# Weights and a context chunk loaded in 32 by 32 blocks and turned by VectorE, in the first stage of an attention kernel

## The reference

```python
x = x + _L0_xattn_ref(_layernorm(x, axis=-1), ctx_1024, ctx_1024, wq, bq, wk, bk, wv, bv, wo, bo)
...
    q = (query @ wq.T + bq).reshape(B, SQ, H, HD).transpose(0, 2, 1, 3)
    k = (key @ wk.T + bk).reshape(B, -1, H, HD).transpose(0, 2, 1, 3)
    v = (value @ wv.T + bv).reshape(B, -1, H, HD).transpose(0, 2, 1, 3)
    scores = jnp.einsum('bhqd,bhkd->bhqk', q, k) / jnp.sqrt(jnp.asarray(HD, q.dtype))
    attn = jax.nn.softmax(scores, axis=-1)
...
x = x + _L0_attn_ref(_layernorm(x, axis=-1), ...)
x = x + _L0_ffn_ref(_layernorm(x, axis=-1), ...)
```

## Time and profile before

| | |
|---|---|
| time, median of 3 runs | 1691.88 us (1691.49 to 1692.56) |
| profiled execution: its time | 1690.8 us |
| profiled execution: span from the first to the last instruction | 1689.0 us |
| TensorE matmul busy | 1619.8 us, 96% |
| VectorE, ScalarE, GpSimd busy | 1179.0, 950.8, 899.7 us |
| first stage: first transpose, first product, last eviction | 6.50, 14.55, 69.57 us |
| mean granted TensorE clock | 0.973 |

### The profile page before, as it was taken

One profiled execution on the slowest core, in us unless ns is written; L12 is line 12 of the kernel. 1 busy time (PEld: TensorE's weight loads), 2 busy tenths in 40 slices (PEclk: granted clock), 3 DMA queues, 4 the chain that ended last, 5 costly groups with the idle time before them and its releaser, 6 DMA issues. The chain is left out here.

```text
span 1689.0 us, 36984 instructions
## 1 busy us (share of the span) xinstructions
PE 1619.8 (96%) x15589; PEld 1314.5 (78%) x15604; DVE 1179.0 (70%) x1523; ACT 950.8 (56%) x1437; POOL 899.7 (53%) x472
## 2 busy tenths in 40 slices
PE   7999999999999999999999999667998899999999
PEld 6788888888888888888888887556886677777787
DVE  5137888888888888888888887877434577653322
ACT  4347776777767777777777776662103677630000
POOL 0026788888878878888887885002000344522220
PEclk9999999999999999999999999788999799899999
DMA  5332222222222222222222210213422111211001
GB/s 187 75 50 35 36 39 40 39 38 37 38 37 42 36 36 40 41 36 37 37 40 37 40 24 5 80 53 113 165 88 94 38 51 51 65 50 50 28 23 50
DMA packets 310404, 88.75 MB, mean 53 GB/s; under 512 B 259392, under 2 KB 292160, under 8 KB 310240
## 3 DMA queue, kind: packets, MB, share of 16 engines
q1 hardware_dynamic: 310240, 86.39, 22.2%
HBM read 71.67 MB, written 14.68 MB: 51 GB/s over the span
## 5 line engine op out<-in xcount | busy, mean ns | idle before, releaser
L655 POOL TENSOR_TENSOR b_acc<-b_acc,b_s 128x1024 f32<-128x1024 f32 x168 | 563.6, 3355 | 12.4 <-ACT b_s L854 5.3
L892 DVE TENSOR_TENSOR b_s<-b_s,b_mb 128x2048 f32<-128x2048 f32 x128 | 398.0, 3111 | 28.4 <-ACT b_mb L837 28.4
L929 DVE TENSOR_TENSOR b_mx<-b_psS,b_mx 128x512 f32<-128x512 f32 x480 | 330.8, 689 | 93.3 <-PE b_psS L720 80.2
L854 ACT ACTIVATE b_s<-b_s 128x2048 f32<-128x2048 f32 x128 | 244.3, 1909 | 18.3 <-DVE b_s L892 15.2
L871 ACT ACTIVATE b_s<-b_psS 128x2048 f32<-128x2048 f32 x128 | 241.2, 1885 | 20.9 <-DVE b_mx L929 20.9
L43 PE MATMUL b_work<-wvT,cT 128*128 128x512 f32 x496 | 202.9, 409 | 0.0
L43 PE MATMUL b_work<-cT,wkT 128*128 128x512 f32 x496 | 200.3, 404 | 1.7 <-POOL b_ones L636 1.7
L44 PE MATMUL b_work<-wvT,cT 128*128 128x512 f32 x496 | 194.5, 392 | 0.0
L44 PE MATMUL b_work<-cT,wkT 128*128 128x512 f32 x496 | 194.2, 392 | 0.0
L45 PE MATMUL b_work<-wvT,cT 128*128 128x512 f32 x496 | 193.8, 391 | 0.0
L45 PE MATMUL b_work<-cT,wkT 128*128 128x512 f32 x496 | 193.4, 390 | 0.0
(11 more groups left out here) (290 smaller groups left out, 2802.4 us busy)
## 6 DMA issues: line engine op xcount, KB each, us to landing
cin<-in_ctx SPq DMA_DIRECT2D x480, 64.0 KB, 2.4
experts_sb<-in_L_ffn_expert_w SPq DMA_DIRECT2D x8, 1024.0 KB, 5.3
q_scratch<-d_st SPq DMA_DIRECT2D x16, 256.0 KB, 2.3
k_scratch<-d_st SPq DMA_DIRECT2D x16, 256.0 KB, 2.3
e_q<-q_scratch SPq DMA_DIRECT2D x16, 256.0 KB, 2.7
k_sb<-k_scratch SPq DMA_DIRECT2D x16, 256.0 KB, 2.9
cin<-in_ctx SPq DMA_DIRECT2D x4, 512.0 KB, 8.4
b_kT<-in_x SPq DMA_DIRECT2D x4, 512.0 KB, 8.0
```

Source lines behind the costliest of these rows:

```text
L655: nc.gpsimd.tensor_tensor(acc[:, :, :], acc[:, :, :], s[:, buf, 2 * i:2 * i + 2, :], ALU.add).then_inc(sum_done, 1)
L854: nc.scalar.activation(part, part, ACT.Exp, scale=SCALE).then_inc(exp_done, 1)
L892: nc.vector.tensor_tensor(s[:, n % BUFS, :, :], s[:, n % BUFS, :, :], mb[:, :].rearrange("p (o n) -> p o n", o=1).broadcast_to([P, CHUNK, ...
L929: nc.vector.tensor_tensor(mx[:, :, :], part, mx[:, :, :], ALU.max).then_inc(mx_done, 1)
```

## The change

The units `("w", 1, k)`, `("w", 2, k)` and `("c", 1, n)` leave `order`. Instead twelve `blocks` (four of wv, four of wq, four of chunk 1) are each loaded with four DMAs by `load_blocks`, turned by VectorE (`turn`) into one of four places in the buffer of wk, copied to the high half by ScalarE at the places that `ahead` lists, and subtracted by GpSimd. The loads of x move ahead of those of wv, and the two bias loads stand behind the sixteen DMAs of wv. VectorE now does all statistics, the rest of the norm and the turning of wv before the normalization of half 0. The square root on ScalarE moves up to the second key unit.

```diff
-        order = ([("w", 0, k) for k in range(KD)] + [("c", 0, n) for n in range(4)]
-                 + [("k", 0, 0), ("w", 1, 0), ("w", 1, 1), ("k", 0, 1), ("w", 1, 2), ("w", 1, 3),
-                    ("k", 0, 2), ("c", 1, 0), ("c", 1, 1), ("k", 0, 3), ("v", 0, 0), ("c", 1, 2), ("c", 1, 3),
-                    ("v", 0, 1), ("w", 2, 0), ("w", 2, 1), ("x", 0, 0), ("x", 0, 1), ("v", 0, 2),
-                    ("w", 2, 2), ("w", 2, 3), ("x", 0, 2), ("x", 0, 3), ("v", 0, 3),
+        order = ([("w", 0, k) for k in range(KD)] + [("c", 0, n) for n in range(4)]
+                 + [("k", 0, j) for j in range(G)] + [("v", 0, 0), ("v", 0, 1), ("x", 0, 0), ("x", 0, 1), ("v", 0, 2),
+                    ("x", 0, 2), ("x", 0, 3), ("v", 0, 3),
...
+        blocks = [("w", 1, k) for k in range(KD)] + [("w", 2, k) for k in range(KD)] + [("c", 1, k) for k in range(KD)]
+        ahead = {("k", 0, 2): blocks[0:2], ("k", 0, 3): blocks[2:4], ("v", 0, 2): blocks[4:6], ("v", 0, 3): blocks[6:8],
+                 ("q", 0, 1): blocks[8:10], ("q", 0, 2): blocks[10:12]}
...
-            load_weights(1)
+            for g in range(G):
+                sp.dma_start(parts[:, g, 1:3, :], x[2 * g:2 * g + 2].rearrange("b p d -> p b d")).then_inc(x_in[g // 2], 16)
+            for u in blocks[0:KD]:
+                load_turned(u)
...
         @block.gpsimd
         def _(pool):
             make_identity(nc, pool, ident, const)
+            for u in blocks:
+                kind, done, count = (("w", w_lo, w_hi), ("c", shared.split_done, shared.hi_done))[u[0] == "c"]
+                pool.wait_ge(count, counted(*u))
+                nc.gpsimd.tensor_tensor(split_place(1, u), turned_place(u), f32(split_place(0, u)),
+                                        ALU.subtract).then_inc(done, 1)
...
-                if (kind, i, j) == ("c", 1, 2):
+                if (kind, i, j) == ("k", 0, 1):
                     norm.scalar(act)
+                for t in ahead.get((kind, i, j), ()):
+                    act.wait_ge(turned, blocks.index(t) + 1)
+                    nc.scalar.activation(split_place(0, t), turned_place(t),
+                                         ACT.Copy).then_inc(w_hi if t[0] == "w" else shared.hi_done, 1)
...
+            def turn(u):
+                n = blocks.index(u)
+                dve.wait_ge(block_in[n], 16 * 4)
+                if n >= 4:
+                    kind, i, j = blocks[n - 4]
+                    dve.wait_ge(w_lo if kind == "w" else shared.split_done, counted(kind, i, j))
+                nc.vector.transpose(turned_place(u), block_place(u)).then_inc(turned, 1)
...
-                if (kind, i, j) == ("w", 1, 2):
+                if (kind, i, j) == ("k", 0, 0):
                     statistics(0)
-                elif (kind, i, j) == ("c", 1, 0):
                     statistics(1)
-                elif (kind, i, j) == ("c", 1, 2):
                     norm.vector(dve)
                     norm.done(dve)
-                elif (kind, i, j) == ("w", 2, 0):
+                    for t in blocks[0:KD]:
+                        turn(t)
                     applied(0)
-                elif (kind, i, j) == ("w", 2, 2):
+                elif (kind, i, j) == ("v", 0, 1):
                     applied(1)
+                    for t in blocks[KD:2 * KD]:
+                        turn(t)
+                elif (kind, i, j) == ("q", 0, 0):
+                    for t in blocks[2 * KD:]:
+                        turn(t)
```

More of the change, by code:

```diff
@@ L214, in context_place, with load_blocks, chunk_columns @@
     return a[:, p % 2, 2 * kk:2 * kk + 2, h * 2 * P:(h + 1) * 2 * P]
-def load_blocks(sp, ctx_in, cin, raw_in, p, k):
-    rows = ctx_in[p // 4, (p % 4) * 512:(p % 4 + 1) * 512, k * P:(k + 1) * P]
+def load_blocks(sp, rows, out, done):
     blocks = rows.rearrange("(t j) (i c) -> i j t c", j=32, i=4)
     for i in range(4):
-        sp.dma_start(cin[32 * i:32 * i + 32, 0, k % 2, :].rearrange("j (t c) -> j t c", c=32),
-                     blocks[i]).then_inc(raw_in[k % 2], 16)
+        sp.dma_start(out[32 * i:32 * i + 32, :].rearrange("j (t c) -> j t c", c=32), blocks[i]).then_inc(done, 16)
+def chunk_columns(ctx_in, p, k):
+    return ctx_in[p // 4, (p % 4) * 512:(p % 4 + 1) * 512, k * P:(k + 1) * P]
 def two(ps):
@@ L248, in queries_and_first_chunk @@
         const = sem("a_const")
+        block_in = [sem(f"a_block_in{n}") for n in range(3 * KD)]
+        turned = sem("a_turned")
         x_in = [sem(f"a_x_in{i}") for i in range(2)]
@@ L281, in queries_and_first_chunk, with turned_place, split_place, block_place @@
         order_of = {kind: [u for u in order if u[0] == kind] for kind in "wcxkvq"}
+        for kind, i, j in blocks:
+            order_of[kind].append((kind, i, j))
+        def turned_place(u):
+            return w_sb[0][:, blocks.index(u) % 4, :]
+        def split_place(a, u):
+            kind, i, j = u
+            return weights[i][1][a][:, j, :] if kind == "w" else cT[a][:, 1, j, :]
+        def block_place(u):
+            kind, i, j = u
+            return w_sb[i][:, j, :] if kind == "w" else cin[:, j // 2, j % 2, :]
         @block.sync
@@ L287, in load_context, with load_turned @@
                              .rearrange("(o p) d -> p o d", p=P)).then_inc(cin_in[h], 16)
-            def load_weights(i):
-                sp.dma_start(w_sb[i], weights[i][0].rearrange("(o p) d -> p o d", p=P)).then_inc(w_in[i], 16)
-            load_weights(0)
+            def load_turned(u):
+                kind, i, j = u
+                rows = weights[i][0][:, j * P:(j + 1) * P] if kind == "w" else chunk_columns(ctx_in, 1, j)
+                load_blocks(sp, rows, block_place(u), block_in[blocks.index(u)])
+            sp.dma_start(w_sb[0], weights[0][0].rearrange("(o p) d -> p o d", p=P)).then_inc(w_in[0], 16)
             for h in range(2):
                 load_context(0, h)
-            load_weights(1)
+            for g in range(G):
+                sp.dma_start(parts[:, g, 1:3, :], x[2 * g:2 * g + 2].rearrange("b p d -> p b d")).then_inc(x_in[g // 2], 16)
+            for u in blocks[0:KD]:
+                load_turned(u)
             with nc.allow_non_contiguous_dma(reason="512 numbers"):
@@ L298, in _ @@
                 sp.dma_start(bq[:, :], w["bq"].rearrange("(g p) -> p g", p=P)).then_inc(b_in, 16)
[L299 to L305, removed]
+            for u in blocks[KD:2 * KD]:
+                load_turned(u)
+            sp.wait_ge(full, place["c", 0, 3] + 1)
+            for u in blocks[2 * KD:]:
+                load_turned(u)
             for k in range(2):
-                load_blocks(sp, ctx_in, cin, shared.raw_in, 2, k)
+                sp.wait_ge(turned, 2 * KD + k + 1)
+                load_blocks(sp, chunk_columns(ctx_in, 2, k), cin[:, 0, k, :], shared.raw_in[k])
             for n, (_, half, g) in enumerate(order_of["q"]):
@@ L593, in load_queries, with load_chunk @@
                 sp.dma_start(q[:, n % 3, :], q_d[g, b]).then_inc(q_in[n % 3], 16)
+            def load_chunk(p, k):
+                load_blocks(sp, chunk_columns(ctx_in, p, k), cin[:, 0, k % 2, :], shared.raw_in[k % 2])
             for n in range(3):
@@ L597, in _ @@
             sp.wait_ge(turned, 1)
-            load_blocks(sp, ctx_in, cin, shared.raw_in, 2, 2)
+            load_chunk(2, 2)
             for beat in range(FIRST, LAST):
@@ L602, in _ @@
                     sp.wait_ge(turned, u - 2 * CHUNK + 1)
-                    load_blocks(sp, ctx_in, cin, shared.raw_in, *divmod(u + 2, CHUNK))
+                    load_chunk(*divmod(u + 2, CHUNK))
                 n = score_step(beat - 1)
```

## The result

The changed kernel took 1695.82 us (median of 20 runs), the kernel before 1692.26 us (20 runs). The ratio is 1.0018 with a 95% interval of 1.001 to 1.0025: slower by 1.7 to 4.2 us. The forecast was 1697.6, in a range of 1693.0 to 1700.5, slower with a chance of 75%. Direction and range hold; the forecast of +5.7 us is more than half as large again as the 3.6 us by which the medians differ. The profiled execution of the changed kernel has a span of 1694.4 us.

The account below looks back on a forecast made before the run. TensorE, busy 96% of the span, was taken as the bound, through its first-stage timeline. Terms: -7.5 + 9.25 + 2.5 + 1.45 = +5.7 us on 1691.9, giving 1697.6 us, range 1693.0 to 1700.5.

Parts of the forecast that it names:

- The saving on TensorE: First stage: six transposing pairs (5.4 us) and the wait for normalized x (2.1 us) leave TensorE, -7.5 us.
- The biases: Bias loads, behind 23 DMAs, land at 24.1 us instead of 12.6, holding ScalarE's first key eviction.
- The limit of about 2,000 pieces: SP's issue: estimated outstanding limit, letting only three or four block loads issue before x lands at 14.6 us.
- What hangs behind them: After the first key eviction: root, norm, wv turning from 27.4, GpSimd's subtractions to 34.1, first value unit 0.1 later.
- The first wait: TensorE idle between the last key unit and first value unit, 25.5 to 34.8 us: +9.25 us.
- The clock: First value unit after the long wait: matmuls at granted clock 0.50, 1.2 GHz, +2.5 us.
- GpSimd slowed: GpSimd's wv subtractions beside VectorE's normalization of x: 0.6 us taken, from a span of nothing to 1.5.
- the price of 1.5 us on GpSimd: wv subtractions: under an exclusive port lock, each normalization and subtraction would take turns, three times 0.48 us.
- The second wait: Before the first query unit: TensorE waits for the last wq copies and GpSimd's last two subtractions, +1.45 us.
- The rival of the other side: Biases land early and don't hold the root: first value unit at 28.3, -3.2 us, 1688.7 us; chance 8%.

Follow-up runs that it names:

- wv_tensor: Changed kernel, but wv transposed by TensorE, its load and the biases as before the change, wq copies one unit earlier: 1686.52 us, ratio 0.9959.
- bias_first: Changed kernel with the two bias loads issued before the loads of x: 1689.5 us, ratio 0.9987.
- root_first: Changed kernel with ScalarE taking the square root ahead of the first key eviction, biases still late: 1693.29 us.
- kept_warm: Changed kernel with 36 extra matmuls, result overwritten, between the last key unit and the first value unit: median 1693.6 us, upper group 1694.4.
- norm_apart: Changed kernel with VectorE normalizing x only after GpSimd has subtracted all of wv: 1695.27 us.
- wq_early: Changed kernel with VectorE turning wq before the second half of the normalization and ScalarE copying its blocks one unit earlier: 1686.61 us.
- low_vector: bias_first with the four low halves of wv subtracted by VectorE instead of GpSimd: median 1679.72 us, last eviction of the stage at 63.99.
- low_vector_wq: low_vector with wq copies one unit earlier and three wq turnings between the halves of the normalization: 1684.88 us, ratio 0.995.
- all_turned: Changed kernel with biases, then wv blocks ahead of x, wv turned before the statistics, copies one unit earlier, root at first value unit: 1687.66 us.

## Why the prediction was right, and where its sizes were off

- **The saving on TensorE (-7.5).** Right: the transposing pairs and the old wait are gone. wv_tensor showed four of the six pairs and the wait by themselves, as worked out.
- **The biases (24.1).** 23.6. SP was held as estimated: the first five block loads took 9.39 us, where three or four were expected before x has landed, the rest went at 0.53 each, and the last was issued at 20.35, where 21.2 was worked out. The limit of about 2,000 pieces fits this, but no run tested it. That the late biases cause the wait, bias_first showed.
- **What hangs behind them.** Right link by link: the root at 25.67, the first turning at 26.96, the subtractions from 28.42, the first value unit at 34.05 where 34.8 was said. root_first showed a second path that the prediction didn't name, ScalarE's copies behind the key evictions: taking the root out of the chain gives only half of the 6.3 us back that early biases give.
- **The first wait (9.25).** 8.9, if the 25.13 at which the key units end (14.13 + 11.0) is taken from 34.05; 8.79 in the row.
- **The clock (+2.5).** This is the term that was mis-sized most: 1.75 us, by the first value unit's 4.81 against 3.05 in kept_warm. The stretch in the earlier trace rows gave all twelve matmuls at the low level; here the clock rose before the unit was done (0.53 in the window from 36 to 38, and 1.00 from 38 on).
- **GpSimd slowed (+0.6 of it).** 0.56 by norm_apart. The Trainium skill's rule (SBUF — State Buffer, Who interferes with whom), an exclusive port pair between the two engines, says which pair collides, and the trace agrees that this one does; but the price of 1.5 us on GpSimd that I drew from it is not what came: three subtractions met a normalization, as the sum had it, but each lost 0.18 and not 0.48. GpSimd lost 0.56 and VectorE 2.90.
- **The second wait (+1.45).** 1.4, if the 48.6 at which the next matmul would have started is taken from 49.99; 1.22 in the row. wq_early took it away.
- **A term that wasn't there:** the first product started at 14.13 instead of 14.55, since the context transposes of this execution ran faster: sixteen took 2.24 us instead of 2.94. The row of the granted clock has 1.00 for both, so it doesn't say why. It is not an effect of the change: in the nine experiments, in which nothing ahead of it differs, it starts at anything from 13.77 to 14.78.

Together the stage's end moved by 4.26 us: -0.4 - 7.5 + 8.9 + 1.75 + 1.4 = 4.15; the remaining 0.1 I can't assign. Forecast were 5.7, and of the 1.4 too much the clock is 0.75. From the stage's end on the two profiled executions differ by another 1.1 us (a span 5.4 longer), of which 1.0 arises in the last stretch of the second stage (the same score matmuls start 4.26 us later, at 1063.99 against 1059.73, and the next stage's first product 5.26 later, at 1148.51 against 1143.25), where bursts run at either clock level (the mean granted clock from 1060 to 1144 us is 0.78 before and 0.80 after); the change touches nothing there. Over all runs the difference is 3.1 by the ratio and 3.6 by the medians, 0.7 to 1.2 less than the stage's. The later stages vary by as much without any edit of theirs: in the seven traces of the upper group, from the stage's end to the end of the span it is 1619.4 to 1621.0 us. So that the time agrees less well than the stage is no sign for or against a term.

The rival of the other side was right as a mechanism and in its price: with the biases early the first value unit starts at 27.75 (28.3 was said) and the time is 1689.5 (1688.7). It counted on a clock that may stay up, and it fell. In the changed kernel it could not happen: SP was held so long that it issued bk and bq only at 20.40 and 20.93, later than the 19.5 by which they had to land, so no overtaking would have helped.

## What to carry to other kernels

A load of 2 KB can be the most expensive one to move: look up who waits for it, and what stands behind that waiting instruction on its engine, before putting many small-piece DMAs ahead of it. Move work off the bound engine first where its result is needed late: the same idea gained 6.5 us of the stage for wq and chunk 1 and lost 4.3 when wv, needed first, went along. With its order mended (biases early, the low halves of wv by VectorE, wq earlier) the whole change gained 6.9, hardly more than the late part alone. After any wait of TensorE of about two microseconds and more, read the granted clock of what follows, and count it as a term of its own.

## What the runs showed of the hardware that I had not expected

**Two groups of run times, 8 us apart, from a part that nobody changed.** The profiled execution of kept_warm is of the lower group, that of the changed kernel of the upper one. kept_warm's first stage ends 1.97 us earlier, its span is 10.3 us shorter. Of the other 8.3, 1.4 arise before the first product behind cross-attention (1148.5 and 1145.1 us), 2.2 from there to the first product of the stage that follows (1195.4 and 1189.8), and 4.8 in the scores of self-attention. These run from 1299.9 to 1465.6 us in the changed kernel (165.7 us) and from 1294.3 to 1455.2 in kept_warm (160.9). All eleven traces agree in this: the seven of the upper group have 46.8 to 46.9 us and 165.7 to 165.8 for these two stretches, the four of the lower group (kept_warm, low_vector, wq_early, low_vector_wq) 44.5 to 44.7 and 160.9 to 161.0. Windows of 10 us in the scores, the changed kernel:

```profile
1320.00:1330.00 10.00, 6.86 (x59) 6.07 (x60) 5.97 (x19) 7.20 (x36) 3.30 (x5) 0.74 0.20 56
...
1340.00:1350.00 10.00, 7.01 (x62) 5.99 (x62) 7.46 (x20) 6.76 (x34) 4.12 (x8) 0.76 0.15 52
1350.00:1360.00 10.00, 9.78 (x70) 7.64 (x71) 5.01 (x14) 5.71 (x23) 4.01 (x8) 0.73 0.19 54
```

and kept_warm:

```profile
1330.00:1340.00 10.00, 7.08 (x68) 5.53 (x68) 6.81 (x21) 7.13 (x35) 4.04 (x8) 1.00 0.17 54
1340.00:1350.00 10.00, 9.74 (x91) 7.89 (x90) 8.89 (x23) 9.15 (x41) 6.06 (x10) 1.00 0.18 54
1350.00:1360.00 10.00, 10.00 (x80) 7.71 (x80) 7.08 (x20) 7.32 (x36) 3.66 (x8) 1.00 0.16 53
```

The stage of the scores begins with bursts and waits, and in it the clock goes down and up several times; in one execution it settles at 1.00 some 30 us earlier than in the other. How often a kernel falls in the lower group ranges from none in eleven runs (bias_first) to eight in twelve (wq_early). Whether the kernel's timing ahead of it decides or only chance was not tested; the 8 us are larger than most effects studied here, so for a change in one stage the position of the stage's end is to be read beside the time.

**The length of a wait alone doesn't tell whether the clock falls.** It fell after 1.89 us of idling (root_first, at 14.15), 2.28 (all_turned, at 41.08) and 2.51 (bias_first, at 27.75). It stayed up after 0.79 (low_vector) and 1.97 us (before the change), and also after 2.25, in low_vector, where the granted clock is 1.00 from 13 to 15 us:

```profile
13.99 0.47 PE L43 MATMUL a_ps<-cT,wkT 128*128 128x512 f32 x1 [2.25 <-DVE cT L493]
```

What else decides, no run here tells.

**GpSimd's subtractions hardly suffer from VectorE's normalization, and each normalization that meets one takes nearly three times as long** (1.48 us and not 0.54; 6.64 and not 3.74 for the eight of which three did): the engine that one looks at may not be the one that pays.
